# A six-layer local-attention network on one core: k's transposes behind the v projection, the output made inside the last layer

## The reference

```python
x = x + attn1(layernorm(x))             # 16 sequences x 256 tokens x 128, windows of 64, 16 heads of 8
y = layernorm(x)
for i in range(6):                      # 16 heads of 64, windows of 32 looking one window back
    h = shift_tokens(y)                 # the second half of the channels is taken from the token before
    q, k, v = split(h @ Wqkv[i])        # 128 -> 3 x 1024
    q, k = rotary(l2norm(q) * qs), rotary(l2norm(k) * ks)
    y = local_attention(q, k, v) @ Wo[i] + y
    h = shift_tokens(y)
    h = layernorm(h) * g[i] + b[i]
    a, gate = split(h @ W1[i] + b1[i])  # 2 x 341
    y = (a * gelu(gate)) @ W2[i] + b2[i] + y
out = x + y
```

## Time and profile before

| what | value |
|---|---|
| median of three runs | 3418.71 us (3418.09 to 3419.04) |
| the profiled execution | 3418.27 us, its span 3416.5 us |
| busy: PE / DVE / ACT / POOL | 93% / 82% / 76% / 77% of the span |
| mean granted TensorE clock | 0.973 of full speed |
| span 410 to 2880 us, the loop and its lead-in | PE 372.87 of 390 us, then some 496 of every 520 |
| 3396 to 3417 us | PE 8.73 of 21 us, clock 0.50 |

### The profile page before, as it was taken

One profiled execution on the slowest core, in us unless ns is written; L12 is line 12 of the kernel. 1 busy time (PEld: TensorE's weight loads), 2 busy tenths in 40 slices (PEclk: granted clock), 3 DMA queues, 4 the chain that ended last, 5 costly groups with the idle time before them and its releaser, 6 DMA issues.

```text
span 3416.5 us, 133004 instructions
## 1 busy us (share of the span) xinstructions
PE 3188.8 (93%) x52802; PEld 2706.0 (79%) x52802; DVE 2812.1 (82%) x3743; ACT 2597.2 (76%) x3707; POOL 2626.1 (77%) x2593
## 2 busy tenths in 40 slices
PE   7978999989999989999989999989999999999996
PEld 4647888878788878888878888878888878888885
DVE  7967888888788888888888888888878888888882
ACT  6746778877787878778777877878778777878874
POOL 6648888878877878878878878877878887888871
PEclk9979999999999999999999999999999999999997
DMA  1001111111111111111101111111111111111111
GB/s 63 2 10 36 58 39 33 38 28 44 52 43 38 35 31 41 43 56 35 40 27 46 36 58 39 33 33 39 40 59 33 38 35 38 37 40 33 38 35 29
DMA packets 57827, 130.82 MB, mean 38 GB/s; under 512 B 10992, under 2 KB 33136, under 8 KB 56432
## 3 DMA queue, kind: packets, MB, share of 16 engines
q1 hardware_dynamic: 57200, 121.94, 12.2%
HBM read 19.17 MB, written 2.10 MB: 6 GB/s over the span
## 4 chain that ended last, share of the span: by engine, by line
PE 70%; ACT 15%; issue 8%; DVE 5%; POOL 2%; ACTq 0%; DMA 0%; POOLq 0%; DVEq 0%; SPq 0%
PE pair L211 56%; PE pair L214 13%; ACT qT L855 10%; ACT sq L845 3%; DVE ts L977 1%; ACT ss L850 1%; DVE ss L981 1%; DVE mx L998 1%; DVE qk L973 0%; DVE pair L994 0%; DVE tab L955 0%; POOL qk L1080 0%; DVE tab L956 0%; DVE Sx L1002 0%; ACT sq L837 0%
## 5 line engine op out<-in xcount | busy, mean ns | idle before, releaser
L1101 POOL TENSOR_TENSOR qk<-qk,ts 128x1024 f32<-128x1024 f32 x384 | 912.4, 2385 | 228.8 <-DVE ts L977 213.5
L973 DVE TENSOR_TENSOR qk<-pair,tab 128x1024 f32<-128x1024 f32 x384 | 468.2, 1219 | 365.6 <-ACT sq L837 362.8
L1080 POOL TENSOR_TENSOR qk<-qk,rn 128x1024 f32<-128x1024 f32 x384 | 733.1, 1930 | 28.6 <-issue 13.5
L211 PE MATMUL pair<-wq_h,xs_h 128*128 128x512 f32 x1154 | 512.3, 444 | 31.6 <-issue 14.8
L832 ACT ACTIVATE Sx<-Sx 128x1024 f32<-128x1024 f32 x192 | 203.4, 1060 | 395.4 <-DVE Sx L1002 395.4
L214 PE MATMUL pair<-small,qk 128*128 128x128 f32 x3104 | 420.5, 279 | 75.4 <-ACT qT L855 54.5
L1112 POOL TENSOR_TENSOR Sx<-Sx,rden 128x1024 f32<-128x1024 f32 x192 | 365.3, 1902 | 157.2 <-DVE rden L1032 157.2
L211 PE MATMUL pair<-wq_h,xs_l 128*128 128x512 f32 x1152 | 469.7, 408 | 0.4
L211 PE MATMUL pair<-wq_l,xs_h 128*128 128x512 f32 x1152 | 468.4, 407 | 0.0
L977 DVE TENSOR_TENSOR ts<-pair,tab 128x1024 f32<-128x1024 f32 x384 | 466.0, 1214 | 0.0
L981 DVE TENSOR_REDUCE ss<-sq 128x16 f32<-128x1024 f32 x384 | 463.9, 1208 | 0.0
(11 more groups left out here) (126 smaller groups left out, 6678.6 us busy)
## 6 DMA issues: line engine op xcount, KB each, us to landing
VB<-VA SPq DMA_DIRECT2D x192, 384.0 KB, 3.5
VB<-VA SPq DMA_DIRECT2D x96, 128.0 KB, 3.5
wq_raw<-wqkv SPq DMA_DIRECT2D x6, 1536.0 KB, 7.2
xf<-xT SPq DMA_DIRECT2D x96, 64.0 KB, 1.9
xf<-xT SPq DMA_DIRECT2D x96, 63.8 KB, 2.0
wo_sb<-wo SPq DMA_DIRECT2D x6, 512.0 KB, 3.6
X<-x_in SPq DMA_DIRECT2D x4, 512.0 KB, 7.6
out<-X SPq DMA_DIRECT2D x8, 256.0 KB, 2.3
```

The source lines that it names most:

```text
L211: return T_.matmul(out, lhsT, rhs, start=start, stop=stop, **k)
L973: V_.tensor_tensor(h3(qk[:, now, kind, :], DH), h3(source[:, :], DH), rep(tab[:, 2 * kind, b, :], HEADS, DH), ALU.mult)
L1080: G_.tensor_tensor(x, x, bc(rn[:, then, kind * HEADS:(kind + 1) * HEADS], HEADS, DH), ALU.mult).then_inc(S["scaled"], 1)
L1101: G_.tensor_tensor(qk[:, now, kind, :], qk[:, now, kind, :], ts[:, kind, :], ALU.add).then_inc(S["added"], 1)
```

## The change

In TensorE's step the transposes of k (second use of PC) come behind the v projection instead of ahead of it, and in ScalarE's step the copy to kT (L865) comes behind the copy to VA (L872). In odd steps the transposes of xf come behind w2 and the transposes back. `finish`, its meeting and the group constants are gone: in the last turn, from t = 13 on in odd steps, TensorE transposes sequence q of xT (read in place) into the second half of bank0, VectorE adds it to X1 behind the update L1039, and the q projection of the next even step waits for that add. SP stores sixteen pieces of 256 tokens after its steps. The values of FILL and FILL_AHEAD are the same in both kernels.

```diff
@@ step_pe
             if pl.has(0):
                 ...
+                if pl.last and pl.seq(14) is not None:
+                    e.wait_ge(S["o_sum"], pl.seq(14) + 1)
                 ...
                 last.then_inc(S["av_done"], 1)
+            if pl.has(0):
+                e.wait_ge(S["rotated"], blocks(pl, "rotated", 0, 1))
+                if fresh:
+                    e.wait_ge(S["wq_low_v"], layers(pl, 1, t // NBLOCKS, 1))
+                project(e, t, one, high, low, 2 * INNER).then_inc(S["v_done"], 1)
+                fill(e, t, 17)
             if pl.has(1):
                 e.wait_ge(S["scaled"], blocks(pl, "scaled", 1, 2))
                 e.wait_ge(S["qkT_kept"], blocks(pl, "qkT_kept", 1, 1))
                 for a in range(PAIRS):
                     last = tr(PC[:, a * P:(a + 1) * P], qk[:, then, 1, a * P:(a + 1) * P])
                 last.then_inc(S["qkT_done"], 1)
-            if pl.has(0):
-                (the same v projection)
                 ...
-            q = pl.seq(5)
-            (transposes of xf, now behind those of f_xn)
+            q = pl.seq(13)
+            if pl.last and q is not None:
+                e.wait_ge(S["x_done"], seqs(pl, "x_done", SEQS + q, 1))
+                if pl.has(0):
+                    e.wait_ge(S["rotated"], blocks(pl, "rotated", 0, 2))
+                elif q:
+                    e.wait_ge(S["o_sum"], q)
                 for h in range(BLOCKS):
+                    last = tr(bank0[:, LEN + h * P:LEN + (h + 1) * P], xT[:, q * LEN + h * P:q * LEN + (h + 1) * P])
+                last.then_inc(S["o_t"], 1)
@@ step_act: the copy to kT (L865) behind the copy to VA (L872)
@@ step_dve, behind the update of x (L1039)
+            q = pl.seq(13)
+            if pl.last and q is not None:
+                e.wait_ge(S["o_t"], q + 1)
+                new = X1[:, q * BLOCKS:(q + 1) * BLOCKS, :]
+                V_.tensor_tensor(new, new, h3(bank0[:, LEN:2 * LEN], P), ALU.add).then_inc(S["o_sum"], 1)
@@ sync
-            for i in range(GROUPS):
-                sp.wait_ge(S["o_sum"], i + 2)
-                sp.dma_start(o[:, i * NT:(i + 1) * NT, :], X1[:, i * NT:(i + 1) * NT, :]).then_inc(S["stored"], 16)
+            for q in range(SEQS):
+                sp.wait_ge(S["o_sum"], q + 1)
+                sp.dma_start(o[:, q * BLOCKS:(q + 1) * BLOCKS, :], X1[:, q * BLOCKS:(q + 1) * BLOCKS, :]).then_inc(S["stored"], 16)
```

More of the change, by code:

```diff
@@ L156, in build @@
         S = {n: sem(n) for n in (*STEP, *PER_SEQ, *LOADS, *PARTS, *ONCE, *FIRST, "xf0", "xf1", "vb0", "vb1", "vb2", "vb3", "phase",
-                                 "stored", "opened", "o_copied", "o_t", "o_sum", "zeroed",
+                                 "stored", "opened", "o_t", "o_sum", "zeroed",
                                  "cleared", "waited")}
@@ L165, in give_ahead @@
         def give_ahead(e):
-            for n in ("o_t", "o_sum"):
-                e.sem_inc(S[n], 1)
             e.sem_inc(S["phase"], PHASE_AHEAD)
@@ L762, in step_pe @@
                     last.then_inc(S["w1_done"], 1)
-            q = pl.seq(5)
[L764 to L769, removed]
+            q = pl.seq(13)
[5 more added lines that the diff above has]
+                    e.wait_ge(S["o_sum"], q)
                 for h in range(BLOCKS):
-                    last = tr(bank2[:, h * P:(h + 1) * P], xf[:, q % 2, h * P:(h + 1) * P])
-                last.then_inc(S["turned"], 1)
+                    last = tr(bank0[:, LEN + h * P:LEN + (h + 1) * P], xT[:, q * LEN + h * P:q * LEN + (h + 1) * P])
+                last.then_inc(S["o_t"], 1)
             q = pl.seq(11)
@@ L794, in step_pe @@
                 last.then_inc(S["turned_back"], 1)
+            q = pl.seq(5)
+            if q is not None:
+                e.wait_ge(S[f"xf{q % 2}"], pl.times(SEQS // 2 * 32) + (q // 2 + 1) * 32)
+                if pl.has(1):
+                    e.wait_ge(S["qkT_kept"], blocks(pl, "qkT_kept", 1, 2))
+                elif pl.seq(11) is not None:
+                    e.wait_ge(S["gated"], seqs(pl, "gated", pl.seq(11), 3))
+                for h in range(BLOCKS):
+                    last = tr(bank2[:, h * P:(h + 1) * P], xf[:, q % 2, h * P:(h + 1) * P])
+                last.then_inc(S["turned"], 1)
             if pl.has(1):
@@ L872, in step_act @@
                 A_.activation(VA[:, r, :], one[:, :], ACT.Copy).then_inc(S["v_kept"], 1)
+            if pl.has(1):
+                e.wait_ge(S["qkT_done"], blocks(pl, "qkT_done", 1, 2))
+                bb = (t - 1) % BLOCKS
+                A_.activation(kT[:, :, WIN + bb * P:WIN + (bb + 1) * P], h3(PC[:, :], P), ACT.Copy).then_inc(S["qkT_kept"], 1)
             q = pl.seq(9)
@@ L1182, in shift_values @@
                 sp.dma_start(VB[0:WIN, r, :], VA[P - WIN:P, r - 1, :]).then_inc(done, 16)
-        FT1 = banks[0:2]
-        NT = GROUP // P
-        area = flat(qk[:, :, :, :]).rearrange("p (n c) -> p n c", c=GROUP)
-        o_in = area[:, 0, :]
-        def finish(e, who):
-            with e.Fori(0, GROUPS) as i:
-                if who == "act":
-                    e.wait_ge(S["o_t"], i + 1)
-                    A_.activation(o_in, xT[:, bass.ds(i * GROUP, GROUP)], ACT.Copy).then_inc(S["o_copied"], 1)
-                if who == "pe":
-                    e.wait_ge(S["o_copied"], i + 1)
-                    e.wait_ge(S["o_sum"], i + 1)
-                    for t in range(NT):
-                        last = tr(FT1[0][:, t * P:(t + 1) * P], o_in[:, t * P:(t + 1) * P])
-                    last.then_inc(S["o_t"], 1)
-                if who == "dve":
-                    e.wait_ge(S["o_t"], i + 2)
-                    V_.tensor_tensor(X1[:, bass.ds(i * NT, NT), :], X1[:, bass.ds(i * NT, NT), :],
-                                     h3(FT1[0][:, :], P), ALU.add).then_inc(S["o_sum"], 1)
         def clear(dve):
@@ L1255, in _ @@
             steps(pool, step_pool)
-            meet(pool, 2)
         @block.scalar
```

14 lines of the change are left out of this document (1 added, 13 removed).

## The result

The changed kernel takes 3457.86 us (median of 4 runs, 3452.73 to 3467.93), the kernel before 3418.88 (4 runs) beside it: ratio 1.0115, 95% interval 1.009 to 1.014. The forecast was 3391 us, with a range of 3374 to 3409. The sign is wrong, and the time lies 49 us above the range.

The account below looks back on a forecast made before the run. The prediction took odd halves to be bound by a circle of VectorE and ScalarE that TensorE only keeps up with. Its sum: 3418.3 - 16.1 (A) - 3.4 (B) + 4.0 (C) - 12 (D) = 3390.8 us, range 3374 to 3409.

Parts of the forecast that it names:

- A: After the last update of x: removing the output loop cuts 20.7 us to 4.6, 16.1 won, bounds 14 to 17.
- B: In the drain: w2 and the transposes back no longer stand behind the late turned xf; 3.4 us won, bounds 0 to 3.5.
- C: Output work in the last turn: ten VectorE adds in odd halves without a hole, 4.0 us lost, bounds 2.2 to 7.7.
- D: In the loop: v's projection ahead of k's transposes, winning in t = 2 mod 4; 12 us won, bounds -13.5 to +17.
- the idle times alone: TensorE's idle times around k's transposes: the smaller estimate of the swap's gain per step, 0.15 us, where 0.24 was taken.
- the hole before the gelu: Even half: VectorE idles 0.35 us before the first L1066, waiting for the gelu; forecast to stay.
- the mark against my reasoning: In the loop: a table load over 0.15 us earlier against the copy of o would prove D's reasoning wrong.
- the term for the instructions' delivery: At v's start in even steps: a possible stall of 0.3 us in up to 45 steps, 13.5 us lost.
- the 0.45 us at w1: In t = 2 mod 4: w1's weight load on TensorE stands idle 0.45 us on nothing the profile shows.
- R3: Rival, slower: v starts 0.45 us late every even step, 31 us lost, 3434; chance 0.04, milder forms 0.05.
- E: Unchanged table of empty instructions: counts per step stay, so price 0 beyond D.

Follow-up runs that it names:

- e1: The changed kernel with the swap undone on TensorE and ScalarE, leaving A, B and C: 3398.5 us, ratio 0.9935 to the kernel before.
- e2: The kernel before with only the swap, on TensorE and ScalarE, the turned xf still ahead of w2: 3570.4 us, ratio 1.0441.
- e15: The changed kernel with the new order only in steps t = 3 mod 4, old order in the others: 3383.3 us, ratio 0.9912 to the kernel before.
- e18: As e15, with 8 empty instructions fewer in the first step: 3383.9 us, ratio 0.99 to the kernel before.
- e9: The changed kernel with the steps' table of empty instructions all zeros, the six at the start kept: 3405.9 us, ratio 0.9973 to the kernel before.

## Why the prediction was wrong, by its own steps

- *A, the output loop*: right. 4.6 us of tail forecast, 3.8 measured; 16.8 won for 16.1.
- *B, w2 ahead of the turned xf*: the link is right, that the sum agrees is luck. At t = 35 of the last turn w2 starts where y ends (3421.96), and the next w1 comes 6.0 us behind y's end (3427.93), for 10.4 before: 4.4 us won there, 3.4 forecast. But the first two steps of the drain (t = 192 and 193) are 4.1 us longer than before, and the rest 7.7 shorter, 2.0 of it since the kernel before has a stall of the kind above in t = 194; so -3.5 for -3.4 is a balance of terms that I didn't forecast. e1, with B and C alone, has 70.7 us for 70.9. Over all 16 kernels with B the drain is 62.3 to 73.5 us, mean 67.1. What I said in one clause, that "in odd steps xf was put last for that", is worth more than all of B's own price: without it a step t = 1 mod 4 is 1.14 us longer (e2).
- *C*: right in size. The ten odd steps of the last turn are 15.52 for 15.18 where no stall is in them, 0.34 each, 3.4 us for 4.0; the add takes 0.41.
- *D, the swap*: the wrong step. Its direct part was right in kind and half the size: t = 2 mod 4 is 10.1 us shorter in 40 steps, but e1, without the swap, has 4.0 of these, so the swap's own is 6.1 us, 0.15 a step (the figure of "the idle times alone"), for the 12 that I took. VectorE's waits there went as forecast, 15.3 us to none, and the steps still kept most of it. t = 0 and 1 mod 4 gain nothing; the hole before the gelu stays. The table load came 3.51 us after the copy of o started, 3.75 before: 0.24 earlier, beyond the 0.15 that I had set as the mark against my reasoning, and yet nothing was won from it, since the hole behind it grew (0.49 for 0.35). What failed is the term for the instructions' delivery: "0.3 us in up to 45 even steps", with the bounds "-13.5 and +17", sized by the 0.45 us at w1. In its place stood a stall of 1.2 to 1.75 us in each fourth step, which made it 0.9 us longer where the clock stayed up and 2.6 to 3.2 us where it fell: 53.8 us in these steps and 61 in all against e1.
- *R3, the rival for slower*, looked at the right 2 us ("v's projection now follows the attention products at once. These are 256 instructions in 2 us") and took the wrong object: it let v start late in each even step, where the stall is inside the products of the odd step after, and the price comes from a block that lands late, in 13 of 30 steps more than doubled by the clock. Against it I set that "inside the products no idle time shows now". That is true of the loop and false of the trace, which has this stall in the drain, 4 us ahead of the rows that I read there:

```profile
3352.92 0.18 PEld L211 LDWEIGHTS pair<-PT,VB 64*64 64x64 f32 x1 [1.88 <-issue]
```

  And for the loop it was no evidence: in t = 3 mod 4 the block was there only some 1.1 us ahead of need (3.74 for 4.9), and the trace has the packets' starts, which I didn't read. 0.04 was far too little.
- *The rule on blocks.* The Trainium skill (Runtime: NRT & Kernel Launch, Instruction fetch mechanics) has the next page fetched while the current one runs, hidden because instructions are issued more slowly than they are fetched. I used that rule only to price w1's stall. The traces disagree for TensorE's short products: 256 instructions in 2.0 us, against some 2.5 us from the start of a fetch to its use.
- *E, the table of empty instructions*, "Price 0 beyond D": the counts are the same, but their purpose depends on the order they pad. The same table with the new order is at a bad place; with 48 more at the start the kernel takes 44 us less.

## What to carry to other kernels

When a kernel's instruction stream is as dense as here, read the instruction queue as one more engine: where its packets start, and how long ahead of use. An exchange of two neighbours that changes no count and no duration can still move a fetch; try it with the boundaries shifted by 16, 32 and 48 instructions before it is judged. Search the whole trace for the stall before you say that it isn't there. And an exchange that is bad as a whole may be good in one step of four: e15 and e18 win 0.9 and 1.0% against the kernel before.

## What the runs showed of the hardware

- A stall of TensorE at the boundary of 256 instructions ends 1.39 us after a packet of 16,384 bytes has landed on q8 (kernel after), with medians of 1.35 to 1.44 in all profiles. That it waits for just this packet is inferred from that constancy.
- An empty instruction (a semaphore increment) follows another in TensorE's stream after 0.15 us. In the projections of the kernel after, weight loads start 0.23 us apart with none or one of them in between, 0.25 with two and 0.45 with three (medians). Even steps are shorter without the table (e9).
- In t = 87 TensorE stood still for 1.61 us and then ran some 3.4 us at the granted clock 0.50. The echo cost more than the stall: at the same stall of 1.20 us a step had 16.2 us without the fall and 17.9 with it, for 15.34 with neither.
- Small VectorE operations, 0.28 us each by themselves, took 1.98 to 2.42 us beside a GpSimd multiply at the layer change (kernel before and e15), and two that took 2.37 us together in e15 took 4.12 in the kernel before.
